# A cap on the gathers under way: each indirect DMA waits for the landing of the one four before it

## The reference

```python
flows = jnp.einsum('bchw,koc->kbohw', x, Woff) + boff[:, None, :, None, None]
weights = jax.nn.softmax(logits, axis=1)
out = gather(x0i, y0i, wx0 * wy0) + gather(x1i, y0i, wx1 * wy0) + gather(x0i, y1i, wx0 * wy1) + gather(x1i, y1i, wx1 * wy1)
out = jnp.einsum('kbohw,bkhw->bohw', feats, weights)
```

## Time and profile before

| what | value |
|---|---|
| time, median of 3 runs | 715.41 us (712.96 to 718.45) |
| profiled execution, first to last instruction | 712.8 us |
| PE busy | 612.1 us (86%) |
| DVE busy | 550.0 us (77%) |
| ACT busy | 362.1 us (51%) |
| POOL busy | 363.5 us (51%) |
| HBM read and written | 168.05 MB and 28.51 MB |
| mean granted clock of TensorE | 0.919 |

### The profile page before, as it was taken

One profiled execution on the slowest core, in us unless ns is written; L12 is line 12 of the kernel. 1 busy time (PEld: TensorE's weight loads), 2 busy tenths in 40 slices (PEclk: granted clock), 3 DMA queues, 4 the chain that ended last, 5 costly groups with the idle time before them and its releaser, 6 DMA issues.

```text
span 712.8 us, 10744 instructions
## 1 busy us (share of the span) xinstructions
PE 612.1 (86%) x3020; PEld 488.4 (69%) x3029; DVE 550.0 (77%) x1316; ACT 362.1 (51%) x892; POOL 363.5 (51%) x385
## 2 busy tenths in 40 slices
PE   1999799999997897798989797978979977888888
PEld 0444475778886776586868686867868866676777
DVE  6999774579998739595789685969687859786796
ACT  0298885789985442352443654335364426234242
POOL 0030593235554475465656565656665655556640
PEclk9999899999999567797999998999998999899999
DMA  9900001127777798799999999999999998999992
GB/s 358 369 22 1 0 1 54 44 84 210 211 211 237 243 371 303 291 354 387 358 352 364 381 345 376 346 360 373 364 379 360 358 371 301 367 394 360 368 368 60
DMA packets 77366, 197.04 MB, mean 276 GB/s; under 512 B 7337, under 2 KB 36812, under 8 KB 77196
## 3 DMA queue, kind: packets, MB, share of 16 engines
q0 software_dynamic: 43488, 154.55, 59.0%
q1 hardware_dynamic: 33836, 42.03, 17.0%
HBM read 168.05 MB, written 28.51 MB: 276 GB/s over the span
## 4 chain that ended last, share of the span: by engine, by line
PE 40%; DVE 10%; issue 10%; another core or an unknown queue 5%; ACT 2%; POOL 0%; DVEq 0%
PE ps L1534 24%; PE ps L1559 7%; DVE ps L1164 5%; PE ps L1561 4%; PE ps L1484 2%; PE ps L1547 2%; ACT v L1311 1%; DVE ps L1161 1%; DVE wvs L1171 0%; DVE wvs L1164 0%; DVE xs L1178 0%; DVE wq L1171 0%; PE ps L1594 0%; DVE wq L1164 0%
## 5 line engine op out<-in xcount | busy, mean ns | idle before, releaser
L954 POOL DMA_INDIRECT v<-table,index x252 | 236.2, 937 | 151.4 <-issue 62.8
L1534 PE MATMUL ps<-v 128*128 128x256 f32 x786 | 209.3, 414 | 35.9 <-issue 28.0
L1164 DVE SCALAR_TENSOR_TENSOR ps<-v,weights,ps 128x256 f32<-128x256 f32 x489 | 215.3, 486 | 2.6 <-DVE ps L1161 1.0
L1534 PEld LDWEIGHTS ps<-v 128*128 128x128 f32 x786 | 157.4, 209 | 67.2 <-issue 37.3
L1311 ACT ACTIVATE v<-ident,weights 128x128 f32<-128x128 f32 x464 | 139.2, 388 | 8.7 <-remote 5.9
L1324 ACT COPY pick_mask<-ps 128x512 f32<-128x512 f32 x18 | 10.5, 585 | 133.4 <-remote 84.6
L1403 PE MATMUL ps<-wq,s_ring 128*128 128x256 f32 x288 | 68.1, 380 | 1.5 <-ACT ps L1247 0.9
L941 POOL TENSOR_TENSOR xs<-xs,v 128x512 f32<-128x512 f32 x36 | 45.1, 1276 | 46.6 <-DVE v L1011 46.6
L1324 ACT COPY sample<-ps 128x512 f32<-128x512 f32 x17 | 10.0, 585 | 114.6 <-remote 73.7
L1403 PEld LDWEIGHTS ps<-wq,s_ring 128*128 128x128 f32 x288 | 53.9, 191 | 9.4 <-issue 2.9
L488 ACT ACTIVATE a_ring<-xs,small 128x768 f32<-128x768 f32 x48 | 49.0, 1026 | 10.2 <-POOL t_ring L475 5.2
(11 more groups left out here) (174 smaller groups left out, 971.2 us busy)
## 6 DMA issues: line engine op xcount, KB each, us to landing
table<-stage SPq DMA_DIRECT2D x72, 256.0 KB, 3.2
xs<-in_x_dram SPq DMA_DIRECT2D x11, 768.0 KB, 11.3
out_dram<-xs SPq DMA_DIRECT2D x28, 256.0 KB
v<-table,index POOLq DMA_INDIRECT x252
early<-const_syn POOLq DMA_DIRECT2D x18, 192.0 KB, 3.8
ana<-const_ana SPq DMA_DIRECT2D x1, 2304.0 KB, 20.0
out_dram<-xs SPq DMA_DIRECT2D x7, 238.0 KB
stage<-table,index POOLq DMA_INDIRECT x36
```

Source lines behind the costliest of these rows:

```text
L954: nc.gpsimd.indirect_dma_start(places[a], None, table, bass.IndirectOffsetOnAxis(ap=index[:, t, k:k + 1], axis=0)) \
L1164: V.scalar_tensor_tensor(to, corner, weight, ps[:, DVE_SUM, i * C:(i + 1) * C], ALU.mult, ALU.add).then_inc(added, 1)
L1534: m = T.matmul(ps[:, PE_SUM[i], 0:C], diag[2 * u + i][n], places[a][:, q * C:(q + 1) * C], start=n == 0, stop=n == len(mine) - 1)
```

## The change

Every gather of a tile after the first waits in addition until the gather of the same head of the tile before has landed. That one was issued four gathers earlier.

```diff
                                 if t >= RING:
                                     pool.wait_ge(added, added_by(t - RING, last_of_head(t - RING, k)))
                                     pool.wait_ge(used, used_by(t - RING, k))
+                                if t > 0:
+                                    pool.wait_ge(landed[place_of(t - 1, k)], 16 * use_of(t - 1))
                                 nc.gpsimd.indirect_dma_start(places[a], None, table,
                                                              bass.IndirectOffsetOnAxis(ap=index[:, t, k:k + 1], axis=0)) \
                                     .then_inc(landed[a], 16)
```

## The result

| kernel | median of its runs, us | profiled span, us |
|---|---|---|
| before | 716.93 (712.96 to 720.10, 4 runs) | 712.8 |
| after | 744.23 (742.60 to 748.55, 4 runs) | 741.7 |

The ratio is 1.0415, with an interval of 1.0367 to 1.0463. The forecast was 706 us with a range to 730; it has the wrong sign. The same two kernels on another chip took 666.24 and 748.10 us, 1.122 times (1.1166 to 1.1274). From the first gather to the last the changed kernel takes 478.5 us here and 479.4 there; it is the kernel before that differs.

A forecast was written before the change was run, and what follows sets the result against it. The prediction took late PE signals, held up while gathers fill the DMA engines, to stall DVE and GpSimd. 712.8 less 9 gave 703.8 us; plus 2.6 to the median, 706 us, range 684 to 730.

The forecast's parts named there:

- The bound: Third stage: late PE semaphore signals stall DVE, then GpSimd, while gathers fill the DMA engines; DVE's waits total 82 us.
- the correlation on which I said the forecast hangs: Third stage, one trace: PE signals 11.7 and 5.8 us late while DMA engines are full, arriving as transfers drain.
- I cost a met wait at 0: GpSimd's new wait instruction, when already satisfied: 0 us, bounds 0 and 0.05 us each, at most 14 us.
- Under the cap four are shared out over one round trip: Gather pace in the third stage: (5.2 + 0.3 + 0.5) / 4 = 1.50 us, against 1.544 us on average now.
- the release: GpSimd's time from a release to the start of the waiting gather: 0.27 us, taken as 0.3.
- the point where it tips: Gather round trip with everything at which capped pace equals today's: 4 x 1.544 = 6.2 us, against a forecast 6.0.
- The upper end, 1.61 us: Slow end of the capped gather pace, 0.524 / 0.325, from the DMA rate with a short queue.
- the lateness itself: Lateness of a gather's landing signal: taken as 0.5 us, bounds 0 and 5.8 us.
- the slower rival: Landing wait replaces GpSimd's wait for places, and GpSimd pays the round trip serially: 729 us, chance 0.25.
- The lead at the end: Tail behind the last gather issue: of 23.8 us, about 6 are ring lead that would be used up.
- I take half, 9 us: Gain from fewer late PE signals at DVE: half of the 18.4 us possible before gathers bind.
- The rule that spoke against the change: Skill's DMA bandwidth: 341 GB/s for 1 MB, 425 for 16 MB; gives 1.54 us per gather and a change of 0.

The follow-up runs named there:

- b2: The kernel before, unchanged, run again on a quicker chip for its own trace; 667.54 us.
- halfb: The kernel before with each gather writing only the first half of its place, 256 KB in place of 512 KB; 713.53 us, 1.0008 times.
- n6: The changed kernel with gather n waiting for gather n-6 to land, at most six under way; 711.31 us, 1.0016 times the kernel before.
- n8: The changed kernel with gather n waiting for gather n-8 to land; 711.44 us, 1.0024 times the kernel before.
- q6: At most six gathers under way, run later on a chip of the first kind; 710.23 us, 0.9998 times the kernel before.
- a2: The changed kernel, unchanged, run again on a quicker chip; 748.10 us, 1.122 times the kernel before.
- pace320: The kernel before, no landing wait, with a 128x320 scratch fill by GpSimd ahead of each gather; 710.78 us, 0.9969 times.
- pace512: The kernel before, no landing wait, with a 128x512 scratch fill by GpSimd ahead of each gather; 746.48 us, 1.0437 times.
- halfa: The changed kernel with each gather writing only the first half of its place, 256 KB; 711.62 us, 0.9981 times.
- q3: Gather n waits for gather n-3, at most three under way; 847.73 us, 1.1875 times the kernel before.
- t2: The kernel before with gathers of 64 bytes into each partition in place of 4096, on a quicker chip; 623.54 us, 0.9349 times.
- pace16: The kernel before, no landing wait, with a 128x16 scratch fill by GpSimd ahead of each gather; 712.15 us, 1.0032 times.
- rows64: The kernel before with each gather fetching rows for 64 partitions in place of 128, on a quicker chip; 640.61 us, ratio 0.9603.
- h2: The kernel before with each gather writing half its place, 256 KB, on a quicker chip; 625.19 us, 0.9377 times.

## Why the prediction was wrong

**The bound: half right.** That DVE waited for PE signals which PE had long sent, and that a cap would change that, holds: 82 us of such waits fell to some 18, of which 13 are at line 1079. The semaphores' own times, read under b2, show the signals late. That full DMA engines delay them, the correlation on which I said the forecast hangs, is wrong twice over: on one kind of chip the signals are late at a share of 0.65 (halfb), on the other they are in time at 1.03 (b2). Two stretches of one trace, one with much traffic and one with little, differed in everything else too.

**"I cost a met wait at 0": right.** n6, n8 and q6 lie within 0.3% of the kernel before, their intervals around 1.

**"Under the cap four are shared out over one round trip": the right form, and the term that failed is the release in it.** I put 5.2 us for the round trip, 0.3 for the release and 0.5 for the signal, 6.0 in all, and named 6.2 as the point where it tips. Pace times four is 6.68 us. The trace of a2 has all 4608 increments of the landings, and by them the sum closes: from issue to landing, the signal in it, 5.88 us on average, where I had 5.7; from that landing to the start of the gather that waits for it 0.80 us, where I had 0.3. Of the 284 gathers with such a wait 255 start 0.77 us after the landing, so the release is neither 0.3 us nor a matter of a few uneven landings. I had read 0.27 us from a gather that waited for DVE's add, and took it for a gather that waits for a landing. Here the instruction that waits for the landing ends 0.70 us ahead of the gather in 251 of 272 cases; why that takes longer than the release of rows 11 is not shown. With 5.7 + 0.8 = 6.5 the sum alone would have told 1.62 us a gather and a loss.

**The upper end, 1.61 us, was no bound.** I took the rate of the DMA engines in a stretch with a short queue, 325 GB/s. A capped loop is not held by a rate but by latency, and its rate can be any (271 GB/s with three). I had given the lateness itself bounds of 0 and 5.8 us, and did not carry the high one into the pace: even 1.5 us of it gives 1.75. So the slower rival, right that the landing wait takes the place of the wait for places and that GpSimd pays the round trip, was priced at 729 us in place of 744, and the range ended at 730.

**The lead at the end: right.** I took 6 us off the tail; it shrank by 7.3.

**"I take half, 9 us": wrong.** The late signals went nearly whole, and it was worth nothing, since the wait that takes their place ends later.

**The rule that spoke against the change: right in its direction.** The Trainium skill (DMA: Bandwidth & Descriptors, Measured) finds less bandwidth in small transfers. The runs order themselves so: 271 GB/s with three gathers under way, 334 with four, 407 with twelve. By its 341 GB/s my estimate was 1.54 us and no change; the measured pace is 1.67.

**What stays open:** why PE's signals are late on one kind of chip. It needs gathers that come every 1.5 us or faster (pace320, not pace512) and does not need their full bytes (halfb) or more than four under way (halfa). Whether gathers of a few bytes or fills in their place bring it about was tried on chips of the second kind only.

One thing goes with it. Of the 4608 increments of the landings the traces with late signals have recorded between 1258 and 1930 (the kernel before 1598, pace320 1930, halfa 1258); on the same kind of chip those without late signals have 3208 (after), 3984 (pace512) and 4168 (q3); on the second kind every trace has all but a few. So the signals are late where the record of semaphores is full of holes. Every time on record comes with a profiled span, so whether the recording itself has a part in the lateness, or both have one cause, can't be told from these runs.

## What to carry to other kernels

A cap on transfers under way sets a pace of (issue to landing, plus landing to the next issue) / depth, whatever the engines can carry. Compute it with each term at its high end, read the second term from a wait of the same form or bound it, and compare the pace with the one that the consumer has now, before anything that the cap may heal. Price a stall that a change would remove at what remains once the next wait in line is in place. And where a stall has no cause in the trace, take the kernel's trace on a second chip before building on it: here the same program differed by 47 us.

## What the runs showed of the hardware

Chips differ by more than any edit that was meant to be kept: the kernel before takes 709 to 717 us on those of the first kind and 666 on the two of the second, with the same traffic in a burst. What differs is what DVE waits for: 82 us for PE's signals at the three lines and no landing on the first (before), 47 us for landings and 8.5 for PE on the second (b2). GpSimd alone gives a floor of 1.25 us for gathers back to back, of which 0.94 is the instruction and 0.30 idle, whether they fetch 8 KB (t2) or 512 KB (before); a fill of 0.13 us between them is free (pace16). A gather of 64 rows in place of 128 keeps GpSimd 0.90 us, nearly as long, and its 256 KB leave the DMA engines fuller than 256 KB over 128 rows do (rows64, then h2):

```profile
300.00:590.00 290.00, 276.19 (x1460) 230.94 (x1461) 263.67 (x694) 151.92 (x482) 203.69 (x228) 1.00 1.05 229
```

```profile
300.00:590.00 290.00, 278.91 (x1524) 246.36 (x1523) 272.61 (x721) 158.52 (x503) 219.37 (x232) 0.99 0.80 237
```

The share is 1.05 against 0.80 at the same rate of bytes.
